# Flamingo gated cross-attention with a mixture of experts: routing of three batches moved into the second layer, expert regions of 2048 rows, the last projection in the last group's gaps, and the first layer's fills dealt anew

## The chip, the cores and the metric

The kernel runs on one core of a Trainium2 chip. The metric is the device time of that core in microseconds (us) for one execution. Lower is better. Everything is in float32.

## What is computed

The stream `x` is 4 batches of 512 tokens of 256 numbers, the context 4 batches of 512 rows of 512 numbers. Each of four parts adds `tanh(gate) * part(layernorm(x))` to the stream. Cut to what matters:

```
x = x + tanh(g_xattn[0]) * _L0_xattn_ref(_layernorm(x), ctx, ...)   # 16 heads of 16, 512 own keys and 512 of the context
x = x + tanh(g_ffn[0])   * _L0_ffn_ref(_layernorm(x), ...)          # 64 units of 16 hidden values, relu
x = x + tanh(g_xattn[1]) * _L1_xattn_ref(_layernorm(x), ctx, ...)   # 16 heads of 64, 512 context keys and a null key; layernorm of the result
x = x + tanh(g_ffn[1])   * _L1_ffn_ref(_layernorm(x), ...)          # 8 experts of width 1024, the best 2 for each token

def _L1_ffn_ref(X, Wg, bg, W1, W2, W3):
    logits = einsum('btd,de->bte', X, Wg) + bg
    topv, topi = top_k(logits, 2);  w = softmax(topv);  xs = X * w        # one scaled row for each choice
    out = X + sum over e of  where(topi == e, (silu(xs @ W1[e]) * (xs @ W3[e])) @ W2[e], 0)
```

## The kernel before, in words

Three functions run one after the other; each is a block in which the five engines have streams of their own that meet at semaphores. PE is the matrix engine, DVE, ACT and POOL the three others, SP issues loads. T is 4, the number of 128-token tiles of a batch.

**`layer0`.** The 16 heads of a batch are worked in quads of 4, 16 quads in all (q = 0 to 15), each in 8 steps (kt) of 2 halves (c). Before a quad's exponentials its row maxima are needed: `max_scores` computes scores into one of two PSUM banks and `take_max` on DVE reads them, 32 times for each quad, so 512 maxima. The first quad's 32 stand ahead of all its scores. In the steps of quad q, PE computes scores (L348), ACT takes exponentials (L474), PE multiplies them with the values (L363), and the maxima of quad q + 1 run between. What else must be done for later quads and for the batch before is a *fill*: projections of queries and keys (`qk`), values (`v`), transposes into the layouts that the scores need (`q`, `k`), transposes of the result (`oT`), the output projection (`out`), the norm's transposes (`xT`, `xT2`), the unit network (`sin`, `ffn`). A table `slots[(q, kt, c)]`, written by rule, says after which half step a fill is issued. A fill's PSUM bank is free when ACT or DVE has read the fill before it. `q = -1`, `-2` and `-3` are the prologue. Norm statistics of batch 1 stand in the prologue, too.

**`layer1`.** 32 groups (i), 8 to a batch, each of two heads, in 4 steps (r). In each step PE issues: scores of the next group, `scores(i + 1, r)`; a fill at `(i, r, 0)`; 8 transposes of this group's probabilities, `transpose_probs(i, r)`; a fill at `(i, r, 1)`; `weigh_values` of the step before. There is one bank for all fills, so each fill waits until ACT (`misc_act`) or DVE (`misc_dve`) has read the one before. The norm of a batch after its attention (`route_tokens`, into `routed_xn`) is spread over later groups for the first three batches. After the last group `project_output` forms the last batch's projection, 8 head pairs and the null key for each of 4 tiles, and DVE does the norm of it (`output_statistics`, `norm_output`), adds it (`add_output`, L1248).

**`experts`.** A first block norms the last batch again (L61 to L87 on `moe_stats`), transposes all 16 tiles (L1515), forms the logits (L1502) and clears `moe_sorted_x`, the DRAM array of rows sorted by expert (23 tiles of 256 rows). A second block ranks the experts for all tiles (L1529 to L1541), counts the rows of each expert with two matmuls and a prefix sum (L1565, L1566), gives each row its slot and adds the residual (L1605), while ACT scales the first choice's rows (L1614). In a third block ACT scales the second choice's rows (L1775), POOL writes 32 blocks of 128 rows to `moe_sorted_x` by indirect DMA (L1856), SP loads weights (L1679, L1681: 3 DMAs to a piece, 8 pieces of slots) and, when the rows are scattered, the first tiles of rows (L1689). Then come 23 tiles of 8 steps; each weight and each row is split in a high and a low part (`hi`, `lo`), and a product is three matmuls (L1726, L1740). Results go to `moe_y` by indirect DMA (L1862), addressed by token and choice. A fourth block loads both results of each token (L1889), adds them to the stream (L1901, L1903) and writes the output (L1913).

## Time and profile before

| | |
|---|---|
| median of the runs | 2056.9 us (3 runs, 2053.74 to 2070.22) |
| the profiled execution | 2059.87 us |
| its span | 2058.2 us, mean granted PE clock 0.938 |
| PE busy | 1794.1 us (87%) |
| DVE, ACT, POOL busy | 1174.3, 1112.4, 435.1 us |
| layer 0 | 0 to about 690 us |
| layer 1 | about 690 to 1523 us |
| routing, scatter, first weights | 1523 to 1616 us |
| expert tiles | 1616 to 2026 us |
| results and output | 2026 to 2058 us |

The profile is of one execution. The span is what the profiler saw, 1.7 us less than the time that the same execution took; other times in the text are positions from the span's start. An engine's busy time counts its compute instructions. Where an engine was idle the profile names what released it.

### The profile page before, as it was taken

What the parts mean: (1) busy time and instruction counts of PE and PEld (TensorE: products, weight loads), DVE (VectorE), ACT (ScalarE), POOL (GpSimd) and SP (SyncE); (2) the same over time, 40 slices, a digit from 0 to 9 for tenths busy, and PEclk for the clock granted to TensorE, in tenths of its full rate; (3) what the DMA queues carried; (4) which work ended last, traced back from release to release, by engine and by line L of the source; (5) the groups of instructions that cost most, each with busy time, mean ns of one, the idle gap of its engine ahead of it and who ended that gap; (6) DMA issues with size and microseconds to landing.
All of it is one profiled execution on the core that took longest, in us unless ns stands there. A gap on an engine that the chain in (4) does not pass through costs nothing. (4 is left out here: it accounts for less than half of the span.)

```text
span 2058.2 us, 27842 instructions
## 1 busy us (share of the span) xinstructions
PE 1794.1 (87%) x9504; PEld 1125.6 (55%) x9504; DVE 1174.3 (57%) x2825; ACT 1112.4 (54%) x2328; POOL 435.1 (21%) x429
## 2 busy tenths in 40 slices
PE   6899998998997599999999999999870699999993
PEld 3455554554543244444444444454360699999993
DVE  4767777776782455545564556445534355555553
ACT  2366665666665255544554455455513477766771
POOL 3010210110101000000000000000013677777761
PEclk8699999999999799999999999999975799999997
DMA  2000000000000400000000000000035566666644
GB/s 92 1 21 1 11 11 1 2 20 1 0 1 1 149 0 1 21 1 0 1 21 1 1 0 21 1 1 1 1 124 176 176 208 213 208 205 208 206 136 136
DMA packets 112109, 122.42 MB, mean 59 GB/s; under 512 B 9249, under 2 KB 105889, under 8 KB 111969
## 3 DMA queue, kind: packets, MB, share of 16 engines
q1 hardware_dynamic: 104944, 107.76, 16.7%
q0 software_dynamic: 3744, 10.49, 1.4%
q10 hardware_dynamic: 3280, 2.40, 0.4%
q8 instruction: 77, 1.26, 0.3%
q14 instruction: 64, 0.52, 0.1%
HBM read 101.63 MB, written 18.99 MB: 59 GB/s over the span
## 5 line engine op out<-in xcount | busy, mean ns | idle before, releaser
L613 DVE TENSOR_REDUCE l_tile_max<-psum 128x1 f32<-128x512 f32 x512 | 343.9, 690 | 114.7 <-PE psum L333 113.3
L474 ACT ACTIVATE l_probs<-psum 128x1024 f32<-128x1024 f32 x256 | 248.2, 1022 | 104.1 <-PE psum L348 99.9
L333 PE MATMUL psum<-l_kT,l_qT 128*128 128x512 f32 x512 | 245.8, 485 | 37.8 <-DVE l_tile_max L613 33.5
L1848 POOL TENSOR_TENSOR moe_w_lo<-moe_w,moe_w_hi 128x512 fp32r<-128x512 f32 x184 | 241.5, 1313 | 116.3 <-ACT moe_w_hi L1766 115.6
L1190 DVE TENSOR_REDUCE l_row_max<-psum 128x2 f32<-128x1024 f32 x128 | 156.5, 1223 | 162.5 <-PE psum L942 162.2
L1102 ACT ACTIVATE l_null_p<-l_s_null,l_neg_max 128x1 f32<-128x1 f32 x256 | 73.8, 288 | 278.9 <-DVE l_neg_max L1192 278.9
L1726 PE MATMUL psum<-moe_xs_hi,moe_w_hi 128*128 128x256 f32 x736 | 210.9, 287 | 1.4 <-DVE moe_xs_lo L1804 1.4
L1726 PE MATMUL psum<-moe_xs_lo,moe_w_hi 128*128 128x256 f32 x736 | 208.9, 284 | 0.0
L1726 PE MATMUL psum<-moe_xs_hi,moe_w_lo 128*128 128x256 f32 x736 | 208.9, 284 | 0.0
L1829 DVE TENSOR_TENSOR psum<-psum,moe_gate 128x256 f32<-128x256 f32 x184 | 79.4, 432 | 165.0 <-ACT moe_gate L1784 165.0
L333 PEld LDWEIGHTS psum<-l_kT,l_qT 128*128 128x128 f32 x512 | 100.9, 197 | 129.7 <-DVE l_tile_max L613 109.6
L1104 ACT ACTIVATE l_probs<-psum,l_neg_max 128x512 f32<-128x512 f32 x256 | 171.7, 671 | 0.0
L348 PE MATMUL psum<-l_qT,l_kT 128*128 128x512 f32 x512 | 162.0, 400 | 1.8 <-ACT l_probs L474 1.7
L1047 PEld LDWEIGHTS psum<-ident,l_probs 128*128 128x128 f32 x1024 | 119.9, 142 | 70.9 <-issue 52.7
L970 PE MATMUL psum<-l_wv,l_ctxT 128*128 128x512 f32 x256 | 129.8, 654 | 20.4 <-ACT l_null_pT L1130 7.3
L942 PE MATMUL psum<-l_k_sb,l_q_sb 64*128 64x512 f32 x512 | 144.7, 642 | 0.0
L1726 PEld LDWEIGHTS psum<-moe_xs_hi,moe_w_hi 128*128 128x128 f32 x736 | 141.9, 193 | 1.8 <-DVE moe_xs_lo L1804 1.8
L1726 PEld LDWEIGHTS psum<-moe_xs_lo,moe_w_hi 128*128 128x128 f32 x736 | 142.0, 193 | 0.0
L1726 PEld LDWEIGHTS psum<-moe_xs_hi,moe_w_lo 128*128 128x128 f32 x736 | 141.8, 193 | 0.0
L1047 PE MATMUL psum<-ident,l_probs 128*128 128x128 f32 x1024 | 134.7, 275 | 7.9 <-DVE l_probs L1204 5.0
L1061 PE MATMUL psum<-l_probsT,l_v_sb 128*64 128x512 f32 x512 | 140.8, 629 | 0.1
L1784 ACT ACTIVATE moe_gate<-psum 128x256 f32<-128x256 f32 x184 | 70.7, 384 | 127.2 <-PE psum L1726 127.2
(245 smaller groups left out, 3234.7 us busy)
## 6 DMA issues: line engine op xcount, KB each, us to landing
moe_w<-in_moe_w SPq DMA_DIRECT2D x276, 256.0 KB, 4.3
moe_sorted_x<-moe_zeros SPq DMA_DIRECT2D x1, 6256.0 KB, 20.5
moe_xs<-moe_sorted_x SPq DMA_DIRECT2D x23, 272.0 KB
l_ctxT<-in_ctxT SPq DMA_DIRECT2D x4, 1024.0 KB, 5.5
x_resid<-in_x SPq DMA_DIRECT2D x4, 512.0 KB, 10.8
l_raw<-in_ctx SPq DMA_DIRECT2D x4, 512.0 KB, 3.6
l_v_raw<-in_ctx SPq DMA_DIRECT2D x4, 512.0 KB, 3.5
l_wk<-in_wkv SPq DMA_DIRECT2D x1, 2048.0 KB, 16.3
```

Of the source, the lines that this page charges most:

```text
L333: nc.tensor.matmul(bank(4 + m % 2), qT[:, q % SLOTS, h, t * P:(t + 1) * P], kT[:, q % SLOTS, h // 2, half * BANK:(half + 1) * BANK], start ...
L348: last = nc.tensor.matmul(bank(2 * (n % 2) + i), kT[:, q % SLOTS, c, kt * P:(kt + 1) * P], qT[:, q % SLOTS, 2 * c + i, :], start=True, sto ...
L474: nc.scalar.activation(probs[:, n % PT_RING], wide(2 * (n % 2)), ACT.Exp, scale=SCALE).then_inc(exp_done, 1)
L613: nc.vector.reduce_max(tile_max[:, q % 2, t, h, half:half + 1], bank(4 + m % 2), AX_X).then_inc(max_read, 1)
L942: last = nc.tensor.matmul(bank(2 * (t % 2) + j), q_sb[head, i % 2, t * P:(t + 1) * P], k_sb[head, i % 2, :], start=True, stop=True)
L970: last = nc.tensor.matmul(bank(MISC), ctxT[:, c, kt * P:(kt + 1) * P], wv[:, c, half * BANK:(half + 1) * BANK], start=(c == 0), stop=(c == ...
L1047: last = nc.tensor.transpose(bank(4 + j)[:, t * P:(t + 1) * P], probs[:, i % 2, t, j, kt * P:(kt + 1) * P], ident[:])
L1061: last = nc.tensor.matmul(bank(O_BANK)[j * DH:(j + 1) * DH, :], v_sb[:, kt, h * DH:(h + 1) * DH], probsT[:, m % 2, j, :], start=(kt == 0), ...
L1104: last = nc.scalar.activation(probs[:, i % 2, t, j, :], bank(2 * (t % 2) + j), ACT.Exp, bias=neg_max[:, t, j:j + 1], scale=SCALE, accum_ou ...
L1190: nc.vector.reduce_max(row_max[:, t, :], wide(2 * (t % 2)).rearrange("p (j m) -> p j m", j=2), AX_X)
L1726: last = nc.tensor.matmul(bank(k % 3)[:, n * ROWS:(n + 1) * ROWS], w, x_part[:, i % 2, c, :], start=(c == 0 and j == 0), stop=(c == s.DC - ...
L1848: nc.gpsimd.tensor_tensor(w13_lo[:, k % SPLITS], w13[:, slot_k, :, cols], w13_hi[:, k % SPLITS].bitcast(F32), ALU.subtract).then_inc(w13_s ...
```

## The change

**Layer 0.** The table is dealt anew: the four `k` fills of a quad move to kt 0, 1, 3, 4, the first `q` fill of quad q + 3 to (q, 7, 0), the `xT`, `qk`, `xT2`, `sin` and the second `out` fill to later half steps; `UNIT_AT` (the unit network on POOL and DVE) starts 2 steps later. The first 32 maxima use six banks in turn, and the prologue's fills two instead of six. The statistics of batch 1 move from the prologue into quad 0. The `v` fills of the prologue come after the first maxima.

**Layer 1.** New fills `rT` (2), `logits` and `prefix` route batches 0, 1 and 2 inside the layer: for batch 0 in groups 15, 16, 17 and 19, for batch 1 in groups 23, 24, 25 and 27, for batch 2 in groups 30 and 31. DVE ranks the experts of one batch at a time, ACT scales its rows, POOL scatters 8 blocks for each batch. Each expert has a region of 2048 rows of `moe_sorted_x`, so a row's slot needs only the running count of its expert (`run`); the array grows from 46 to 130 blocks of 128 rows and is cleared at the start of layer 1. In the last group 7 of 8 head pairs of the projection of tiles 0 to 3 stand between the last steps; the eighth pair and the null key follow after the last `weigh_values`. The last batch's norm, logits and slots follow in the same block, with the output norm in two fused operations for each tile.

**Experts.** The two routing blocks are gone. DVE turns the counts into a list of tiles, each with its expert and its first row (`list_tiles`), before SP may load weights; SP reads a tile's first row from `start_ids`. POOL scatters the last batch's 8 blocks. DVE instead of POOL splits the first five `w13` weights. The loads of the results stand in the same block, behind the wait for the stores of `moe_y` on SP and ACT.

```diff
 # layer0
-    UNIT_AT = ((2, 1), (2, 3), (2, 4), (2, 4), (2, 5), (2, 6), (2, 7), (3, 0))
+    UNIT_AT = ((2, 3), (2, 4), (2, 4), (2, 5), (2, 6), (2, 7), (3, 0), (3, 0))
...
         if 0 <= q + 2 < NQ:
-            slots[q, 0, 0] = ("q", q + 2, 0)
-            for k, at in enumerate(((1, 0), (2, 1), (3, 0), (4, 0))):
-                slots[(q,) + at] = ("k", q + 2, k)
+            slots.update({(q, kt, 0): ("k", q + 2, k) for k, kt in enumerate((0, 1, 3, 4))})
             slots[q, 5, 0] = ("q", q + 2, 1)
...
+        if 0 <= q + 3 < NQ:
+            slots[q, 7, 0] = ("q", q + 3, 0)
...
         if b + 1 < B and r == 0:
-            slots.update({(q, 7, c): ("xT", b + 1, c) for c in range(2)})
+            slots[q, 7 if b == 0 else 2, 1] = ("xT", b + 1, 0)
         if b + 1 < B and r == 1:
-            slots.update({(q, kt, 1): ("qk", b + 1, t) for t, kt in enumerate((0, 3, 4, 5))})
+            slots[q, 0, 1] = ("xT", b + 1, 1)
+            slots.update({(q, 2 + t, 1): ("qk", b + 1, t) for t in range(T)})
         if b + 1 < B and r == 2:
-            slots.update({(q, 3 + h, 1): ("v", b + 1, h) for h in range(2)})
+            slots.update({(q, (5 if b < 0 else 3) + h, 1): ("v", b + 1, h) for h in range(2)})
         if b >= 1 and r == 0:
             slots.update({(q, 3 + c, 1): ("oT", b - 1, c) for c in range(2)})
-            slots.update({(q, 5 + h, 1): ("out", b - 1, h) for h in range(2)})
+            slots.update({(q, 5 + 2 * h, 1): ("out", b - 1, h) for h in range(2)})
         if b >= 1 and r == 1:
-            slots.update({(q, 7, c): ("xT2", b - 1, c) for c in range(2)})
+            slots[q, 7, 1] = ("xT2", b - 1, 0)
         if b >= 1 and r == 2:
-            slots[q, 0, 1] = ("sin", b - 1)
+            slots[q, 0, 1] = ("xT2", b - 1, 1)
+            slots[q, 2, 1] = ("sin", b - 1)
...
-    START_BANKS, TAIL_BANKS = (MISC, O_BANK, 0, 1, 2, 3), (0, 1, 2, 3, 4, 5)
+    START_BANKS, TAIL_BANKS, FIRST_BANKS = (MISC, O_BANK), (0, 1, 2, 3, 4, 5), (4, 5, 0, 1, 2, 3)
...
-                    if r == 3 and b + 2 < B and kt in (1, 3, 4):
+                    if (r == 3 and 0 <= b < B - 2 or q == 0) and kt in (1, 3, 4):
 # layer1
+    for c in range(ROUTED):
+        first = (c + 1) * PAIRS + PAIRS - 1
+        if c + 1 < ROUTED:
+            at = (first, 0, 1), (first + 1, 0, 1), (first + 2, 0, 1), (first + 4, 0, 1)
+        else:
+            at = (first - 1, 1, 0), (first - 1, 1, 1), (first - 1, 2, 0), (first, 1, 0)
+        slots.update(zip(at, (("rT", c, 0), ("rT", c, 1), ("logits", c), ("prefix", c))))
...
+                clear = g["xs_dram"].rearrange("(n p) d -> p n d", p=P)
+                sp.dma_start(clear, zeros[:].unsqueeze(1).to_broadcast([P, clear.shape[1], WIDE])).then_inc(cleared, 16)
...
+                        if i == GROUPS - 1 and r >= 1:
+                            if r == 1:
+                                pe.wait_ge(exp_done, GROUPS * T)
+                                pe.wait_ge(o_read, GROUPS - 1)
+                            project_heads(bank(r - 1)[:, 0:D], s.B - 1, r - 1, range(PAIRS - 1))
                         if i >= 0 and r >= 1:
                             weigh_values(i, r - 1)
...
+                project_heads(bank(T - 1)[:, 0:D], s.B - 1, T - 1, range(PAIRS - 1))
                 weigh_values(GROUPS - 1, KT - 1)
...
                 for t in range(T):
-                    project_output(bank(t)[:, 0:D], s.B - 1, t).then_inc(out_psum, 1)
+                    if t == 0:
+                        pe.wait_ge(o_read, GROUPS)
+                    project_heads(bank(t)[:, 0:D], s.B - 1, t, (PAIRS - 1,))
+                    project_null(bank(t)[:, 0:D], t).then_inc(out_psum, 1)
 # experts
-                    sp.dma_start(xs[:, i % 2], xs_dram[i * ROWS:(i + 1) * ROWS, :].rearrange("(h p) d -> p h d", p=P)
+                    first = sp.value_load(start_ids[0:1, i:i + 1], min_val=0, max_val=E * s.REGION)
+                    sp.dma_start(xs[:, i % 2], xs_dram[bass.ds(first, ROWS), :].rearrange("(h p) d -> p h d", p=P)
...
+                sp.wait_ge(tiles_ready, 1)
                 for m in range(PIECES):
...
+                all_stored(sp)
+                for b in range(NB):
+                    load_results(sp, 0, b)
...
+                list_tiles()
                 for k in range(AHEAD):
                     split_down(k)
+                    slot_k, cols, _ = arrived(k)
+                    dve.wait_ge(w13_rounded, k + 1)
+                    nc.vector.tensor_tensor(w13_lo[:, k % SPLITS], w13[:, slot_k, :, cols],
+                                            w13_hi[:, k % SPLITS].bitcast(F32), ALU.subtract).then_inc(first_split, 1)
```

**How the order moves, at three places.** On PE in the prologue of layer 0, before (L371 are transposes, L414 the values' projection, L333 the scores for the maxima):

```order
3 L371 MATMUL psum<-ident,l_q_stack 128x128 x4
4 L371 MATMUL psum<-ident,l_k_stack 128x128 x12
5 L414 MATMUL psum<-l_w_qkv,l_xT 128x256 x4
6 L371 MATMUL psum<-ident,l_k_stack 128x128 x4
7 L414 MATMUL psum<-l_w_qkv,l_xT 128x256 x4
8 L333 MATMUL psum<-l_kT,l_qT 128x512 x2
9 L371 MATMUL psum<-ident,l_q_stack 128x128 x4
10 L333 MATMUL psum<-l_kT,l_qT 128x512 x12
11 L371 MATMUL psum<-ident,l_q_stack 128x128 x4
12 L333 MATMUL psum<-l_kT,l_qT 128x512 x4
13 L371 MATMUL psum<-ident,l_k_stack 128x128 x4
14 L333 MATMUL psum<-l_kT,l_qT 128x512 x5
```

and in the changed kernel, where the same three are L380, L423 and L345:

```order
3 L380 MATMUL psum<-ident,l_q_stack 128x128 x4
4 L380 MATMUL psum<-ident,l_k_stack 128x128 x16
5 L345 MATMUL psum<-l_kT,l_qT 128x512 x2
6 L380 MATMUL psum<-ident,l_q_stack 128x128 x4
7 L345 MATMUL psum<-l_kT,l_qT 128x512
8 L423 MATMUL psum<-l_w_qkv,l_xT 128x256 x4
9 L345 MATMUL psum<-l_kT,l_qT 128x512 x4
10 L423 MATMUL psum<-l_w_qkv,l_xT 128x256 x4
11 L345 MATMUL psum<-l_kT,l_qT 128x512 x3
12 L380 MATMUL psum<-ident,l_q_stack 128x128 x4
13 L345 MATMUL psum<-l_kT,l_qT 128x512 x4
14 L380 MATMUL psum<-ident,l_k_stack 128x128 x4
```

Both projections of values now stand behind the first maxima.

On PE in layer 1, group 15, the first of the new fills; before, where L942 are scores, L951 a `q` fill, L1047 the transposes of probabilities and L1061 the weighing:

```order
1276 L1061 MATMUL psum<-l_probsT,l_v_sb 64x512 x2
1277 L942 MATMUL psum<-l_k_sb,l_q_sb 128x512 x2
1278 L951 MATMUL psum<-l_xT,l_wq 128x512 x2
1279 L1047 MATMUL psum<-ident,l_probs 128x128 x8
1280 L1061 MATMUL psum<-l_probsT,l_v_sb 64x512 x2
1281 L942 MATMUL psum<-l_k_sb,l_q_sb 128x512 x2
```

and in the changed kernel, where these are L1000, L1009, L1139 and L1153:

```order
1285 L1153 MATMUL psum<-l_probsT,l_v_sb 64x512 x2
1286 L1000 MATMUL psum<-l_k_sb,l_q_sb 128x512 x2
1287 L1009 MATMUL psum<-l_xT,l_wq 128x512 x2
1288 L1139 MATMUL psum<-ident,l_probs 128x128 x8
1289 L1075 MATMUL psum<-ident,routed_rows 128x128 x4
1290 L1153 MATMUL psum<-l_probsT,l_v_sb 64x512 x2
```

The four transposes of `routed_rows` (L1075) follow the `q` fill with only the 8 transposes between; both use the one bank for fills.

On PE in the last group and behind it, before, from the last group's second transposes (L1006 and L1007 are the projection's head pairs and null key, 8 and 1 to a tile):

```order
1552 L1047 MATMUL psum<-ident,l_probs 128x128 x8
1553 L1061 MATMUL psum<-l_probsT,l_v_sb 64x512 x2
1554 L1047 MATMUL psum<-ident,l_probs 128x128 x8
1555 L1061 MATMUL psum<-l_probsT,l_v_sb 64x512 x2
1556 L1001 MATMUL psum<-ident,l_null_cols 128x128 x4
1557 L1047 MATMUL psum<-ident,l_probs 128x128 x8
1558 L1061 MATMUL psum<-l_probsT,l_v_sb 64x512 x4
1559 L1006 MATMUL psum<-l_wo,l_oT 128x256 x8
1560 L1007 MATMUL psum<-l_w_null_v,l_null_pT 128x256
1561 L1006 MATMUL psum<-l_wo,l_oT 128x256 x8
1562 L1007 MATMUL psum<-l_w_null_v,l_null_pT 128x256
1563 L1006 MATMUL psum<-l_wo,l_oT 128x256 x8
```

and in the changed kernel (L1064 and L1067 are the projection; the routing of the last batch follows it in the same block):

```order
1579 L1139 MATMUL psum<-ident,l_probs 128x128 x8
1580 L1064 MATMUL psum<-l_wo,l_oT 128x256 x7
1581 L1153 MATMUL psum<-l_probsT,l_v_sb 64x512 x2
1582 L1059 MATMUL psum<-ident,l_null_cols 128x128 x4
1583 L1139 MATMUL psum<-ident,l_probs 128x128 x8
1584 L1064 MATMUL psum<-l_wo,l_oT 128x256 x7
1585 L1153 MATMUL psum<-l_probsT,l_v_sb 64x512 x2
1586 L1064 MATMUL psum<-l_wo,l_oT 128x256 x7
1587 L1153 MATMUL psum<-l_probsT,l_v_sb 64x512 x2
1588 L1064 MATMUL psum<-l_wo,l_oT 128x256
1589 L1067 MATMUL psum<-l_w_null_v,l_null_pT 128x256
1590 L1064 MATMUL psum<-l_wo,l_oT 128x256
```

28 of the 32 head-pair matmuls (7 to a tile) now stand between the last group's transposes and weighings, and one pair to a tile behind.

## Rows read from the trace of the kernel before

**Rows 1.** Busy time by window; DMA share and GB/s last.

```profile
core 0: us, PE busy (x) PEld busy (x) DVE busy (x) ACT busy (x) POOL busy (x), PEclk, DMA share, GB/s
38.30:86.00 47.70, 37.40 (x95) 21.77 (x94) 38.09 (x77) 11.10 (x18) 7.65 (x11) 0.57 0.00 0
1140.00:1330.00 190.00, 184.07 (x739) 86.92 (x738) 100.71 (x270) 96.63 (x239) 5.99 (x8) 0.99 0.02 6
1576.00:1584.00 8.00, 0.00 (x0) 0.00 (x0) 1.38 (x4) 2.86 (x7) 6.04 (x7) 0.50 1.08 384
```

**Rows 2.** Waits of PE over the span: us in total, times, longest.

```profile
PE psum L1712 <- DMA moe_xs<-moe_sorted_x: 60.5, 1, 60.5
PE psum L371 <- DVE l_o_tok L658: 9.6, 14, 1.1
PE psum L427 <- DVE l_qT L627: 3.9, 3, 1.3
```

**Rows 3.** Timeline of PE, layer 0: start us, us, instruction, idle before.

```profile
33.38 3.12 PE L414 MATMUL psum<-l_w_qkv,l_xT 128*128 128x256 f32 x8
...
38.32 0.82 PE L333 MATMUL psum<-l_kT,l_qT 128*128 128x512 f32 x2
...
81.23 1.06 PE L348 MATMUL psum<-l_qT,l_kT 128*128 128x512 f32 x2
```

**Rows 4.** The page, costliest groups: busy, mean ns, idle before.

```profile
L613 DVE TENSOR_REDUCE l_tile_max<-psum 128x1 f32<-128x512 f32 x512 | 343.9, 690 | 114.7 <-PE psum L333 113.3
```

**Rows 5.** Timeline of PE in layer 1, groups 14 to 24.

```profile
1059.08 0.66 PE L978 MATMUL psum<-ident,l_rows 128*128 128x128 f32 x4
...
1063.44 1.11 PE L978 MATMUL psum<-ident,l_rows 128*128 128x128 f32 x4 [2.84 <-ACT l_xT L1126]
...
1082.14 1.96 PE L986 MATMUL psum<-l_w_null,l_xT 128*128 128x16 f32 x16
```

**Rows 6.** Timeline around 1450: transposes on PE, the fill read by ACT.

```profile
1448.86 1.04 PE L1047 MATMUL psum<-ident,l_probs 128*128 128x128 f32 x8
...
1450.37 0.59 ACT L1119 ACTIVATE l_q_sb<-psum 128x512 f32<-128x512 f32 x1
```

**Rows 7.** Timeline of DVE in group 30: maxima of consecutive steps.

```profile
1466.74 1.22 DVE L1190 TENSOR_REDUCE l_row_max<-psum 128x2 f32<-128x1024 f32 x1
...
1476.31 1.22 DVE L1190 TENSOR_REDUCE l_row_max<-psum 128x2 f32<-128x1024 f32 x1
```

**Rows 8.** Timeline of PE and DVE behind the last group.

```profile
1497.98 3.69 PE L1006 MATMUL psum<-l_wo,l_oT 128*128 128x256 f32 x16 [0.74 <-issue]
...
1513.86 1.43 DVE L61 BATCH_NORM_STATS2 l_out_stats<-psum 128x6 f32<-128x256 f32 x4 [27.94 <-PE psum L1007]
...
1544.10 0.29 DVE L1485 TENSOR_TENSOR moe_logits<-psum,moe_b_router 128x128 f32<-128x128 f32 x1 [3.73 <-PE psum L1502]
```

**Rows 9.** Groups of DVE, 1498 to 1568: busy us, mean ns, idle before.

```profile
L1536 DVE TENSOR_TENSOR moe_cmp<-moe_cmp,moe_tie 128x1024 f32<-128x1024 f32 x1 | 1.2, 1226 | 0.1
```

**Rows 10.** Timeline at the start of the experts: SP, POOL, PE.

```profile
1568.39 0.91 SPq L1679 DMA_DIRECT2D moe_w<-in_moe_w  x2
...
1608.20 0.96 POOL L1856 DMA_INDIRECT moe_sorted_x<-routed_xn,moe_slot_ids  x1 [0.30 <-issue]
...
1610.65 0.88 SPq L1689 DMA_DIRECT2D moe_xs<-moe_sorted_x  x2
...
1616.01 0.58 PE L1726 MATMUL psum<-moe_xs_hi,moe_w_hi 128*128 128x256 f32 x1 [1.41 <-DVE moe_xs_lo L1804]
```

**Rows 11.** Timeline at the end: the last store and results loads.

```profile
2028.09 0.96 POOL L1862 DMA_INDIRECT moe_y<-moe_y_sb,moe_places  x1 [0.31 <-issue]
...
2037.36 2.83 SPq L1889 DMA_DIRECT2D moe_first_rows<-moe_y  x4
```

**Rows 12.** DMA issues: count, KB each, median us to landing.

```profile
moe_sorted_x<-moe_zeros SPq DMA_DIRECT2D x1, 6256.0 KB, 20.5
...
moe_y<-moe_y_sb,moe_places POOLq DMA_INDIRECT x46, 2.5
```

More of the change, by code:

```diff
@@ L820, in layer1 @@
         slots.update({(i, 3, y): fill for y, fill in late.items()})
+    for c in range(ROUTED):
[5 more added lines that the diff above has]
+        slots.update(zip(at, (("rT", c, 0), ("rT", c, 1), ("logits", c), ("prefix", c))))
     def read_by_dve(fill):
-        return fill[0] in ("k", "null") or fill[0] == "xT" and fill[2] == 1
+        return fill[0] in ("k", "null", "logits", "prefix") or fill[0] == "xT" and fill[2] == 1
     fills = [slots[at] for at in sorted(slots)]
@@ L1159, in _ @@
                             keep_result(i - 1)
+                        route(i, r)
                 keep_result(GROUPS - 1)
+                act.wait_ge(last_psum, 1)
+                nc.scalar.activation(rT[:, 0, :], bank(4), ACT.Copy).then_inc(last_act, 1)
+                weigh_second(s.B - 1)
+                for k in range(TOP):
+                    scale_rows(s.B - 1, k, range(T))
             @block.gpsimd
@@ new lines, in choose_slots, with add_residual @@
+                def choose_slots(c):
+                    dve.wait_ge(scattered, 16 * TOP * T * c)
+                    dve.drain()
+                    for k in range(TOP):
+                        nc.vector.tensor_tensor(chosen[:, k], chosen[:, k], work8[:], ALU.mult)
+                    dve.drain()
+                    nc.vector.reduce_sum(slot[:], chosen[:], AX_X)
+                    dve.drain()
+                    nc.vector.tensor_copy(slot_ids[:], slot[:]).then_inc(slots_ready, 1)
+                def add_residual(c, some):
+                    for t in some:
+                        x_t = tokens(c)[:, t, :]
+                        last = nc.vector.scalar_tensor_tensor(out=x_t, in0=routed[:, t, :], scalar=gates[:, 3:4], in1=x_t,
+                                                              op0=ALU.mult, op1=ALU.add)
+                    if some[-1] == T - 1:
+                        last.then_inc(residual_added, 1)
@@ L1219, in read_fill @@
                         last = nc.vector.tensor_copy(xT[:, rest[1], :], bank(MISC))
+                    elif kind == "logits":
+                        last = add_router_bias(bank(MISC))
+                    elif kind == "prefix":
+                        last = add_counts(rest[0], bank(MISC))
                     else:
@@ L1408, in experts @@
-        row_places = sb("row_places", [P, TILES, HALVES])
+        start_ids = sb("start_ids", [P, TILES], U32)
         places = sb("places", [P, 3, HALVES], U32)
-        rows = (first_rows, xn)
+        results = [sb(f"results_{k}", [P, T, D]) for k in range(TOP)]
         w13 = sb("w13", [P, W_SLOTS, 2 * s.DC, PIECE * P])
         w2 = sb("w2", [P, W_SLOTS, PIECE, D])
-        stats = sb("stats", [P, TB, 6])
-        mv = sb("mv", [P, TB, 2])
-        work = sb("work", [P, 4, TB])
-        norm = Norm(nc, TB, stats, mv, work)
@@ L1771, in round_rows @@
                                          ACT.Copy).then_inc(xs_rounded, 1)
-                for t in range(T):
-                    nc.scalar.activation(xn[:, t, 0:D], xn[:, t, 0:D], ACT.Copy,
-                                         scale=weight[:, 1, t:t + 1]).then_inc(second_scaled, 1)
                 for k in range(AHEAD):
@@ L1791, in _ @@
                         round_rows(i + 1)
+                all_stored(act)
+                for b in range(NB):
+                    load_results(act, 1, b)
             @block.vector
@@ L1840, in _ @@
                 evacuate_y(TILES - 1)
+                for b in range(NB):
+                    dve.wait_ge(results_loaded[b], 16 * TOP)
+                    nc.vector.tensor_tensor(block_rows(results[0], b), block_rows(results[0], b), block_rows(results[1], b),
+                                            ALU.add)
+                    dve.drain()
+                    nc.vector.scalar_tensor_tensor(out=block_rows(g["x"], b), in0=block_rows(results[0], b),
+                                                   scalar=g["gates"][:, 3:4], in1=block_rows(g["x"], b), op0=ALU.mult,
+                                                   op1=ALU.add).then_inc(fin, 1)
             @block.gpsimd
@@ L1935, in flamingo @@
         layer0(nc, s, g, bank, wide, dram)
-        g["routed"] = sb("routed_xn", [P, s.T, s.D + ROW_PAD])
+        g["rows"] = [sb(f"routed_rows_{k}", [P, s.TT, s.D + ROW_PAD]) for k in range(TOP)]
+        g["slot_ids"] = sb("slot_ids", [P, TOP, s.TT], U32)
+        g["run"] = sb("run", [P, s.T + 1, s.E])
+        g["first_slot"] = sb("first_slot", [P, s.E])
+        g["tile_no"] = sb("tile_no", [P, s.TILES])
+        g["steps"] = sb("steps", [P, s.MOST])
+        g["row_places"] = sb("row_places", [P, s.TILES, ROWS // P])
+        g["scattered"] = ctx.enter_context(nc.semaphore("rows_scattered"))
+        xs_dram = nc.dram_tensor("moe_sorted_x", [s.E * s.REGION + ROWS, s.D + ROW_PAD], F32).ap()
+        g["xs_dram"] = xs_dram
         layer1(nc, s, g, bank, wide, dram)
```

625 lines of the change are left out of this document (345 added, 280 removed).

## The prediction

> **What bounds the kernel now.** I read the table of windows first, then PE's waits, then the timeline at each place that the diff touches. PE is busy 87% of the span, so the question is where it is not. Three stretches are PE-bound: layer 0 from 86 us on, layer 1, and the expert tiles. In layer 1 PE is busy 184.07 of 190 us at a granted clock of 0.99 [rows 1]: there an added PE instruction costs its full length, a removed wait gives its full length. Three stretches are not. At the start of layer 0, between the first maxima and the first scores, PE runs at a clock of 0.57 and DVE is busy 38.09 of 47.7 us [rows 1]; both are near their limit. Between the last group and the first expert tile PE works little, and one wait for the first sorted rows is 60.5 us [rows 2]: this is the largest thing in the profile. At the end PE is done by 2026 us and the span goes on to 2058 us.
>
> **The change part by part.** Sums are against the profiled execution, 2059.87 us, which is 3.0 above the median of 2056.9; I come back to that.
>
> *1. Start of layer 0.* Before, 8 of the values' matmuls stood ahead of the first maxima in two runs; the first was 3.12 us beside 4 transposes [rows 3]. They now follow the first three maxima, where PE is filled up to DVE's pace anyway, so the first maximum comes about 3 us sooner. From 38.32 to the first scores at 81.23 [rows 3] were 42.9 us, in which DVE takes 42 maxima at 0.69 us [rows 4] = 29, casts keys and queries (about 4), and computes statistics for batch 1, some 5 us of small instructions. The statistics leave, so DVE needs about 33, and with 6 banks instead of 2 in the ring the two engines hardly wait for each other. PE at its low clock needs about as much. I take 34: 8.9 off, and 3 from the earlier start, less 2.4 given back in quad 0, where the statistics now stand beside maxima at full pace: **−9.5**. Bounds: −14 with nothing given back, −4 if the cold PE sets the pace as before.
>
> *2. Layer 0 in steady state.* PE waits 14 times for DVE's normalised result (L658), 9.6 us in total, since a `tok` fill's reading stands ahead of the next fill; 3 times 1.3 us for `l_qT` before an `out` fill [rows 2]; and about ten times half a microsecond for ACT's copy of a `q` fill before a `qk` or `sin` fill. The new table moves a `k` or a `q` fill away from behind each: I count 7 × 0.65 us, 7 × 0.5, and 3 × 0.8. Against them, the `q` fill that moves to (q, 7, 0) meets DVE's cast and a copy: +2. Sum **−8.4**, bounds −12 and 0 (all waits return elsewhere, since the work of a fill is unchanged and only its neighbours differ).
>
> *3. Fills of batches 0 and 1 in layer 1.* Added to a PE-bound stretch. Work: four transposes took 0.49 us (1059.08 to the next instruction) and sixteen small matmuls 1.81 [rows 5], so a batch costs 2 × 0.49 for `rT`, 1.81 for `logits` and 0.45 for `prefix`: 3.24 us. Waits: each new fill stands at (i, 0, 1) behind a `q` fill with one set of transposes between. PE ended such a set at 1449.9, while ACT read the `q` fill only from 1450.37 for 0.59 us [rows 6], so the new fill could begin only some 1.3 to 1.5 us later. I take 1.4 for all four. Two batches: 2 × (3.24 + 4 × 1.4) = **+17.7**. Bounds: +6.5 without waits; +30 if each wait is like the 2.84 us between two adjacent `xT` fills, after which the next four transposes took 1.11 us instead of 0.66 [rows 5]. I stay nearer the low one because transposes stand between. DVE, ACT and POOL get about 12, 5 and 12 us for each batch, spread over five groups in which they are half idle [rows 1]; free, as long as a probability's chain is not late.
>
> *4. Groups 30 and 31.* Here the last maxima come 4.79 us apart [rows 7], set by the chain maxima, exponentials, normalisation and the small norm steps on DVE, and not by PE; batch 2's fills lie in PE's idle time, but ranking and slots on DVE do not: **+2.6**. In the last group PE is already nearly full. Each tile's 8 pairs took 3.62 to 3.69 us [rows 8], so 7/8 of four tiles = 12.7 us move in front of the last weighing and only 2 to 3 us of idle time is there to be filled, minus slower issue: **−0.8**. This part does hardly anything.
>
> *5. From the projection's end to the first weight load.* Before: 1513.86 [rows 8] to 1568.39 [rows 10], 54.5 us. First the norms, transposes and logits, 30.2 us to 1544.10 [rows 8]. Now: output statistics 4.9, two fused operations for each tile 3.6 (before 4.5), statistics 4.9 with no block's end and no copy before them (some 6 us saved), norm 1.4, no wait for the logits of the other 12 tiles (2.3 saved), transposes, copies and logits 7.0: 21.8, so −8.4. Then 24.2 us of ranks, sums, slots and residual for 16 tiles. The long ranking operations took 1.23 us for 1024 elements [rows 9] and are five; for 256 elements I take 0.5 with the drain: 2.6. Compare 0.9, running counts 1.25, slots 0.95, weights 0.75, residual 1.6, ACT's second scaling behind it 1.6, block's end 0.4, tile list 4.0 and SP's read of it 0.9: 15.0 to 15.6, −8.9. Together **−17.3** (bounds −13, −20).
>
> *6. First weight load to first expert product.* Before: 1568.39 to 1616.01, 47.6 us, set by 32 scatters on POOL, the last at 1608.20; the rows' load at 1610.65 follows and takes 5.4 us to the first product [rows 10]. Now 8 scatters take 10 us and the path is SP's: rows are loaded behind 24 weight loads of 256 KB on the same queue. 6.3 MB and 1.1 MB of scatters at the 384 GB/s of the busiest window [rows 1] are 19.3 us, plus about 4 of ramp, plus 2 for the rows and 2.5 for transposes and split: 27.8. **−19.8**. Bounds: −29 if rows needn't wait for the weights (10.1 + 2.5 + 5.4), −13 if the queue is slower. The new loads from a register's address have no row; weight loads are addressed so already, I add nothing.
>
> *7. Expert tiles.* The same 184 steps of 2.16 us: 0. Splits moved from POOL to DVE are done before the rows arrive.
>
> *8. End.* The last store is issued at 2028.09; a store lands 2.5 us after its issue [rows 12], the loads of the results are issued at 2037.36 [rows 11], after POOL's wait and a block's end. Now SP and ACT wait for the stores themselves: loads at 2030.6, **−6.7** (bounds −1, −7).
>
> *9. The clear of `moe_sorted_x`* grows from 6256 KB, which took 20.5 us [rows 12], to 17,680 KB: 58 us at that pace, but at the start of layer 1, where the DMA engines are all but idle once its weights are in; the next user is batch 1's context. 0, if it doesn't delay `wk`, ahead of it in the queue.
>
> Sum: −9.5 − 8.4 + 17.7 + 2.6 − 0.8 − 17.3 − 19.8 − 6.7 = −42.2, so 2017.7 for the profiled execution, 2014.7 from the median. Forecast **2016**.
>
> **The rivals.**
>
> *A. PE's clock falls in layer 1.* The eight new waits may each be followed by slow instructions, as the 2.84 us wait was (1.11 for 0.66 us [rows 5]). At 1.3 us each: +10, so 2026. Against it: waits of 1.47 us and less were not followed by slow rows in layer 0. The Trainium skill says in "TensorE: Matmul & The Clock Gate", section "A second HAM failure mode: psum-queue depth-cycling", that frequent short idles between matmul groups can make the clock swing; the trace agrees only for waits of over 1.6 us. Chance 0.2.
>
> *B. Start and steady state of layer 0 give nothing*, because cold PE sets the start and waits move to other fills. For it: clock 0.57 [rows 1]. Against: DVE busy 38.09 of 47.7. +14, so 2030. Chance 0.12.
>
> *C. The start of the experts is held by the queue.* Rows behind 24 weight loads and a read of the expert list for each piece; half of term 6 is lost: 2026. The Trainium skill ("DMA: Bandwidth & Descriptors", "Queues, rings and completion order") says that an engine takes turns among queue rows by packets, so scatters and weights share and neither stands still; by it POOL's 8 scatters would not be the delay, while rows on SP's own row still queue. No row here separates the two. Chance 0.1.
>
> *D. Slower than before.* Layer 1's step is PE-bound, so if each new wait left PE at half clock for about half a group (a group is 19.4 us) it would cost 5 us more. It decides from 42/8 = 5.3 us for each of the eight: +48, 2064. Against it: after the 2.84 us wait only the next row or two were slow. Chance 0.03.
>
> *E. The change doesn't do what it says:* the last group has no gaps worth the name (term 4), already in the sum.
>
> **How the numbers follow.** The forecast's own case has 0.55, its bounds put it at 2003 to 2028; A, B and C lie at 2026 to 2030. Cases together (A with B) reach 2036. The range of 8 in 10 is 2001 to 2034. Here 1% (20.6 us) is about what a measurement can tell from no change: faster by more, below 2036, has 0.91; within 1% 0.06; slower 0.03.
>
> **What would show it.** Right: the stretch between the last weighing and the first expert product falls from 119 to about 70 us; PE's wait for the first sorted rows is about 40 us; first scores near 70 us; eight waits of 1.3 to 1.5 us in groups 15 to 27, and a layer 1 that is 15 to 20 us longer up to group 30; results loads about 2 us after the last store. Wrong: a granted clock in layer 1 below 0.95; waits for `l_tile_max` in layer 0 that grow by what the others lost; exponentials late behind the ranking in groups 18 and 26; more than 35 us from the first weight load to the first product.

## The result, and the profile after

The changed kernel takes 2037.9 us (median of 4, 2030.95 to 2043.6), the kernel before 2055.6 (4, 2053.74 to 2070.22): ratio 0.9903, interval 0.988 to 0.9926. So it is 1% faster, 18 to 20 us, where 41 were forecast; the time lies above the range's end of 2034. The profiled execution took 2036.1, its span is 2034.4: 23.8 less than the profiled one of before. 6 us of that difference are the two executions' own: the one of before was 4.3 above its median, this one is 1.8 below.

The table of windows of the changed kernel, beside [rows 1]:

```profile
core 0: us, PE busy (x) PEld busy (x) DVE busy (x) ACT busy (x) POOL busy (x), PEclk, DMA share, GB/s
38.00:86.00 48.00, 37.31 (x163) 23.26 (x161) 41.90 (x78) 19.69 (x27) 7.57 (x11) 0.89 0.00 1
1140.00:1330.00 190.00, 181.00 (x720) 86.47 (x719) 102.46 (x287) 94.30 (x233) 14.40 (x18) 0.96 0.04 12
1580.00:1588.00 8.00, 0.00 (x0) 0.00 (x0) 3.78 (x8) 2.69 (x6) 0.00 (x0) 0.50 1.09 365
```

In the start of layer 0 PE's granted clock is 0.89 and no longer 0.57 (in other executions it is lower, as the experiments show). In layer 1's window PE is busy 181.00 of 190 us instead of 184.07. The weights still load at 365 GB/s. PE's waits, beside [rows 2]:

```profile
PE psum L345 <- DVE l_tile_max L622: 37.6, 37, 2.6
PE psum L1832 <- DMA moe_xs<-moe_sorted_x: 35.6, 1, 35.6
PE psum L1075 <- DVE routed_rows L93: 14.8, 1, 14.8
PE psum L380 <- POOL l_k_stack L600: 5.3, 7, 2.4
PE psum L1075 <- ACT l_q_sb L1227: 4.4, 4, 1.1
PE psum L1075 <- ACT l_rT L1240: 3.1, 1, 3.1
PE psum L380 <- DVE l_o_tok L667: 2.3, 3, 1.0
```

The wait for the first sorted rows fell from 60.5 to 35.6 us, that for `l_o_tok` from 9.6 to 2.3 (another 3.8 us now stand at two other lines). New are the waits of the routing fills (L1075) for `l_q_sb` and for `l_rT`; the one of 14.8 us is the last batch's, whose first transposes now stand in this block behind its norm. The wait for `l_tile_max`, which was 33.5, is 37.6.

Layer 0's start, beside [rows 3]: first maxima at 33.65 instead of 38.32, first scores at 67.43 instead of 81.23.

```profile
33.65 0.73 PE L345 MATMUL psum<-l_kT,l_qT 128*128 128x512 f32 x2 [0.69 <-ACT l_kT L501]
...
67.43 1.00 PE L357 MATMUL psum<-l_qT,l_kT 128*128 128x512 f32 x2
```

Batch 2's second transposes in group 30, and the first transposes of group 31:

```profile
1490.58 0.90 PE L1075 MATMUL psum<-ident,routed_rows 128*128 128x128 f32 x4 [3.09 <-ACT l_rT L1240]
...
1505.37 1.97 PE L1139 MATMUL psum<-ident,l_probs 128*128 128x128 f32 x8 [3.57 <-DVE l_probs L1394]
```

Then the places of [rows 8, 10, 11]: the output statistics, the first weight load, the rows' load and the first expert product, the last store and the loads of the results.

```profile
1535.12 1.42 DVE L67 BATCH_NORM_STATS2 l_out_stats<-psum 128x6 f32<-128x256 f32 x4 [20.72 <-PE psum L1067]
...
1571.69 0.91 SPq L1790 DMA_DIRECT2D moe_w<-in_moe_w  x2
...
1589.32 1.51 SPq L1801 DMA_DIRECT2D moe_xs<-moe_sorted_x  x2
...
1598.26 0.58 PE L1846 MATMUL psum<-moe_xs_hi,moe_w_hi 128*128 128x256 f32 x1 [1.41 <-DVE moe_xs_lo L1923]
...
2011.09 0.96 POOL L2025 DMA_INDIRECT moe_y<-moe_y_sb,moe_places  x1 [0.30 <-issue]
...
2013.50 1.48 SPq L1760 DMA_DIRECT2D moe_results<-moe_y  x3
```

Laid side by side, the positions (us from the span's start) give where the 23.8 us came from. A quad's or a group's "scores" are its first ones, and a quad's last step is the first scores of its kt 7:

| stretch | before | changed | difference | forecast |
|---|---|---|---|---|
| start to scores of quad 1 | 111.5 | 101.2 | −10.2 | −9.5 |
| to quad 15's last step | 529.8 | 529.1 | −0.7 | −8.4 |
| to layer 1's first scores | 68.9 | 74.2 | +5.3 | 0 |
| to the scores of group 31 | 753.5 | 775.0 | +21.5 | +17.7 |
| to the output statistics | 50.2 | 55.7 | +5.5 | +1.8 |
| to the first weight load | 54.5 | 36.5 | −18.0 | −17.3 |
| to the first expert product | 47.7 | 26.6 | −21.1 | −19.8 |
| to the end | 442.1 | 436.1 | −6.0 | −6.7 |

Below the fifth row everything is as forecast. The miss is in layers 0 and 1: +21.4 against +1.6 forecast. How much of it is the change and how much one execution was the question for the experiments.

### The profile page after: what moved, and what is told of

It is laid out like the page before. It is cut to its first block and busy times, and to the rows that moved or that the text cites. A ratio compares the mean times of both kernels' runs of the same rounds, so it can differ in the third digit from the quotient of the medians.

```text
span 2034.4 us, 28113 instructions
## 1 busy us (share of the span) xinstructions
PE 1792.8 (88%) x9516; PEld 1121.3 (55%) x9516; DVE 1181.5 (58%) x2893; ACT 1116.2 (55%) x2334; POOL 423.8 (21%) x430
## 5 line engine op out<-in xcount | busy, mean ns | idle before, releaser
L345 PE MATMUL psum<-l_kT,l_qT 128*128 128x512 f32 x512 | 236.2, 469 | 40.9 <-DVE l_tile_max L622 37.6
L2013 POOL TENSOR_TENSOR moe_w_lo<-moe_w,moe_w_hi 128x512 fp32r<-128x512 f32 x179 | 233.2, 1303 | 139.6 <-ACT moe_w_hi L1886 138.9
L345 PEld LDWEIGHTS psum<-l_kT,l_qT 128*128 128x128 f32 x512 | 98.1, 192 | 131.4 <-DVE l_tile_max L622 110.3
L1139 PEld LDWEIGHTS psum<-ident,l_probs 128*128 128x128 f32 x1024 | 120.4, 142 | 65.5 <-issue 53.6
L1000 PE MATMUL psum<-l_k_sb,l_q_sb 64*128 64x512 f32 x512 | 147.0, 651 | 0.0
L1153 PE MATMUL psum<-l_probsT,l_v_sb 128*64 128x512 f32 x512 | 141.7, 632 | 0.0
L1139 PE MATMUL psum<-ident,l_probs 128*128 128x128 f32 x1024 | 134.8, 275 | 5.7 <-DVE l_probs L1394 5.3
## 6 DMA issues: line engine op xcount, KB each, us to landing
moe_sorted_x<-l_zeros SPq DMA_DIRECT2D x1, 17680.0 KB, 57.1
```

The costliest lines, as they stand in the source:

```text
L345: nc.tensor.matmul(bank(max_bank(m)), qT[:, q % SLOTS, h, t * P:(t + 1) * P], kT[:, q % SLOTS, h // 2, half * BANK:(half + 1) * BANK], sta ...
L1000: last = nc.tensor.matmul(bank(2 * (t % 2) + j), q_sb[head, i % 2, t * P:(t + 1) * P], k_sb[head, i % 2, :], start=True, stop=True)
L1139: last = nc.tensor.transpose(bank(4 + j)[:, t * P:(t + 1) * P], probs[:, i % 2, t, j, kt * P:(kt + 1) * P], ident[:])
L1153: last = nc.tensor.matmul(bank(O_BANK)[j * DH:(j + 1) * DH, :], v_sb[:, kt, h * DH:(h + 1) * DH], probsT[:, m % 2, j, :], start=(kt == 0), ...
L2013: nc.gpsimd.tensor_tensor(w13_lo[:, k % SPLITS], w13[:, slot_k, :, cols], w13_hi[:, k % SPLITS].bitcast(F32), ALU.subtract).then_inc(w13_s ...
```

## The experiments

All times are medians; "the changed kernel" is 2037.9. The kernels of one group ran on one chip beside the kernel before (2055.2, 2058.1 and 2058.4 there; 2060.9, once, beside the changed kernel taken again), so medians of different groups compare to within some 3 us only.

**Layer 0 as before.** The function `layer0` of the kernel before in the changed kernel.

```diff
-def layer0(...):   # the changed one
+def layer0(...):   # the one of before, word for word
```

> The changed kernel with layer 0 as in the kernel before, all else as changed. Theory 1 (all of layer 0's gain is its start: first scores 13.8 us earlier in the trace, 10.2 us of it left at quad 1, and the dealing anew of the later fills is worth 0 to 1 us): the layer reaches the scores of quad 1 at 111 us and of quad 15 at about 615, as before, and the kernel takes 10 to 11 us more than the changed one, about 2048. Rival (the later fills are worth the 8 us that I forecast, and the clock in the tail hid it): 18 us more, about 2056.

2036.1 (2033.76 to 2042.06, ratio 0.9926, 0.9897 to 0.9955, where the changed kernel has 0.9903): not slower by anything that the scatter lets one see. Scores of quad 1 came at 107.9, of quad 15 at 617.2, and layer 1's first scores at 704.1, against 101.2, 611.1 and 704.5. Neither theory had this: in these two traces, the 6.6 us that the new layer 0 has at quad 1 are gone when layer 1 begins.

**The new start, with the later fills as before.**

```diff
-    for q in range(-QUADS, NQ):      # the new table
+    for q in range(-QUADS, 0):       # the new table, q + 3 only for quads 0 and 1
...
+    for q in range(0, NQ):           # the table of before, UNIT_AT and the places in `piece` too
```

> The changed kernel with the new prologue of layer 0, but the fills of quads 0 to 15, the unit network's steps and the places of the output projection's reading dealt as in the kernel before. Theory 1: same as the changed kernel within 2 us, the distance from quad 1 to quad 15 within 1 us of it. Rival: 8 us more, all of it between quad 1 and quad 15.

2039.9 (2033.85 to 2044.68), the same within 2 us. From quad 1 to quad 15's last step 528.9 us with the old table, 529.1 in the changed kernel. That pair hides a little: six of the eight traces of the new layer 0 have 526.3 to 526.5 there, and the one above and the kernel with layer 0 as before, in its two variants, 528.9, 527.8 and 527.9. So the later fills are worth 1.3 to 2.6 us, not 8. The waits say why. Of the kernel with layer 0 as before, in 110 to 630 us:

```profile
PE psum L339 <- DVE l_tile_max L619: 24.7, 25, 2.3
PE psum L377 <- DVE l_o_tok L664: 8.4, 13, 0.7
PE psum L433 <- DVE l_qT L633: 3.9, 3, 1.3
```

and of the changed kernel:

```profile
PE psum L345 <- DVE l_tile_max L622: 28.7, 28, 2.3
PE psum L418 <- DVE l_o_tok L667: 1.9, 3, 0.7
PE psum L444 <- DVE l_o_tok L667: 1.9, 3, 0.7
PE psum L380 <- DVE l_o_tok L667: 1.3, 2, 0.7
```

The waits for DVE's result and for DVE's `l_qT` went from 12.3 to 5.1 us, and the wait for `l_tile_max` rose from 24.7 to 28.7: PE gets sooner to maxima whose bank DVE has not read yet. DVE does the same maxima in the same order, so more than half of what the fills don't wait the maxima do.

**The old start, with the new later fills,** the complement.

```diff
+    for q in range(-QUADS, 0):       # the table of before
...
+    slots[-1, 7, 0] = ("q", 2, 0)    # joins the old table for q < 0 to the new one from q = 0
...
-    START_BANKS, ..., FIRST_BANKS = (MISC, O_BANK), ..., (4, 5, 0, 1, 2, 3)
+    START_BANKS, ... = (MISC, O_BANK, 0, 1, 2, 3), ...   # and batch 1's statistics in the prologue
```

> The changed kernel with the start of layer 0 as before (fills of the prologue, six fill banks, two banks for the maxima, batch 1's statistics in the prologue) and the new dealing from quad 0 on: the complement of the run with the old later fills. Three runs with the new dealing took 74 to 75 us from quad 15's last step to layer 1's first scores, three with the old one 68 to 69, with the same PE instructions in between. Theory 4 (the dealing of the later fills decides when the clock falls in the tail): 74 to 75 us again, and the kernel is about 6 us slower than the changed one with layer 0 of before, 2042. Rival (it is where the tail falls in time, which the start sets): 68 to 69 us and the distance from quad 1 to quad 15's last step at 525 to 529, 2035.

2043.6 (2040.2 to 2048.22): 73.1 us in the tail and 2042 forecast by theory 4, so it looked right. Two kernels of the same group took that back, the one with the head pairs behind the last group and the one with two banks: both have the new dealing, and the tail took 68.9 and 68.6 us. Why this kernel reaches layer 1's first scores at 713.3, the latest of all traces, stays open.

**Two banks for the first maxima.**

```diff
-    ..., FIRST_BANKS = ..., (4, 5, 0, 1, 2, 3)
+    ..., FIRST_BANKS = ..., (4, 5)
```

> The changed kernel with two banks instead of six for the first 32 maxima. Theory 7 (the start was gained by the values' fills and the statistics leaving, and DVE sets the pace): from the first maximum to the first scores 33.8 to 35 us as in the changed kernel. Rival (the hand-over between PE and DVE on two banks was the cost): 37 to 40 us, 3 to 6 more.

From the first maximum to the first scores 41.6 us, in the changed kernel 33.8: 7.8 more, above the rival's 3 to 6 as well. With the old layer 0 it is 40.4 to 42.9. DVE is busy 29.8 us of the 41.6, in the changed kernel 28.8 of the 33.8, so DVE's busy time doesn't set the length. That the hand-over does is not shown, because the granted clock differs too: 0.64 in this start, 0.90 in the changed kernel's. PE is busy 33.5 us instead of 23.7 with the same instructions, while its waits for maxima are 6.1 us instead of 5.3. The changed kernel's two other executions, below, lie between: 37.3 and 37.0 us at 0.73 and 0.78. Whether two banks bring the clock down, or this execution drew a low one, one trace can't tell. The kernel takes 2035.6, no more than the changed one: what the start loses is made up before layer 1, as in the first experiment.

**The changed kernel again, twice.**

> The changed kernel once more, for its trace. Theory 10 (the same instructions meet the clock at another point each time): scores of quad 0, of quad 1 and the tail from quad 15's last step to layer 1's first scores differ between executions of one kernel, as they did between kernels with the same layer 0 (67.4 to 72.1, 101.2 to 107.1 and 68.6 to 75.4 us), and the tail is either near 69 or near 74. Rival (the kernel's own): 67.4, 101.2 and 74.2 within 0.5 us each time.

> The changed kernel a third time, for its trace: as the one before.

2039.9 and 2038.6. First scores at 72.6 and 72.0, scores of quad 1 at 107.6 and 107.1, the tail 68.8 and 68.6 us, where the first execution had 67.4, 101.2 and 74.2. All three numbers differ between executions of one kernel. All traces, in us:

| | first scores | quad 1 | tail | layer 1's first scores |
|---|---|---|---|---|
| old layer 0: before | 81.2 | 111.5 | 68.9 | 710.1 |
| layer 0 as before | 76.9 | 107.9 | 68.4 | 704.1 |
| all three edits, layer 0 as before | 77.5 | 107.9 | 68.7 | 704.5 |
| new layer 0: changed, three times | 67.4, 72.6, 72.0 | 101.2, 107.6, 107.1 | 74.2, 68.8, 68.6 | 704.5, 702.8, 702.0 |
| late fills; rows early | 68.1, 68.1 | 103.0, 103.1 | 75.2, 75.4 | 704.5, 704.8 |
| batch 2 later; heads behind | 67.4, 72.1 | 101.3, 107.1 | 74.1, 68.9 | 704.6, 702.6 |
| all three edits | 70.7 | 105.8 | 68.8 | 700.9 |
| new start, later fills as before | 70.6 | 106.4 | 68.8 | 704.1 |
| old start, new later fills | 80.6 | 112.3 | 73.1 | 713.3 |
| two banks | 75.0 | 110.1 | 68.6 | 705.0 |

Eight traces of the new layer 0 (the last three rows are mixtures) reach layer 1's first scores at 703.3 in the mean, three of the old at 706.2. So the new dealing is worth about 3 us, of 17.9 forecast, and perhaps less: without the trace of the kernel before, at 710.1, the old ones have 704.3. The tail has two lengths, 68 to 69 and 73 to 75. The four traces whose first scores came by 68.1 all have the long one, the five others with the new start and the new later fills (the one with two banks among them) the short one, so what an execution gains early it has lost again by layer 1. In both PE runs the same instructions, at another granted clock (windows of the tail of the changed kernel, the first execution and the second):

```profile
630.00:704.00 74.00, 40.39 (x116) 21.50 (x112) 28.28 (x80) 13.69 (x19) 8.28 (x23) 0.63 0.42 143
```

```profile
634.00:703.00 69.00, 35.31 (x118) 18.55 (x116) 28.34 (x80) 13.52 (x20) 8.31 (x23) 0.73 0.42 144
```

```profile
638.50 6.57 PE L436 MATMUL psum<-l_w_proj,l_oT 128*128 128x256 f32 x16 [0.80 <-ACT l_oT L527]
```

```profile
642.23 3.69 PE L436 MATMUL psum<-l_w_proj,l_oT 128*128 128x256 f32 x16 [0.83 <-ACT l_oT L527]
```

The same output projection takes 6.57 us in the one and 3.69 in the other.

**The routing fills 1 us later.**

```diff
-                        fill((i, r, 1))
+                        routing = slots.get((i, r, 1), ("",))[0] in ("rT", "logits", "prefix") and r == 0
+                        if not routing:
+                            fill((i, r, 1))
...
                         elif i >= 1:
                             weigh_values(i - 1, KT - 1)
+                        if routing:
+                            fill((i, r, 1))
```

> The changed kernel with the eight routing fills at (i, 0, 1) of batches 0 and 1 issued behind weigh_values of the same step instead of ahead of it, 1 us later. Theory 2 (each fill costs a wait of 1.1 to 1.4 us for the read of the q fill, beside 0.5 to 1.8 us of work): the waits shrink to 0.1 to 0.4 us each, layer 1 is 8 to 9 us shorter up to group 30, 2029. Rival (the read of the new fill is then late for the k fill that follows, or the cost is the slower clock): 0 to 2 us less.

2030.2 (2027.31 to 2032.74), 7.7 less, where theory 2 had 8 to 9. In the changed kernel the steps with a new fill are longer than the same steps before by 1.8, 1.8, 3.1 and 1.7 us, for batch 0 as for batch 1: 16.7 together. Here they are longer by 0.8, 0.7, 2.0 and 0.7, 8.6 together, and the step behind `prefix` is longer by 0.5 to 0.9 us. In both kernels the step behind `logits` is longer too, by 1.2 to 1.7 us: in 17 of 20 cases in the ten traces with the fills where the change has them, in 6 of 6 with the late ones. The changed kernel, then this one, at batch 0's `logits` (L1081) and the scores of the next step:

```profile
1146.74 1.95 PE L1081 MATMUL psum<-l_w_router,l_rT 128*128 128x8 f32 x16 [1.10 <-ACT l_q_sb L1227]
...
1149.68 2.08 PE L1000 MATMUL psum<-l_k_sb,l_q_sb 64*128 64x512 f32 x4
```

```profile
1148.84 1.95 PE L1081 MATMUL psum<-l_w_router,l_rT 128*128 128x8 f32 x16
...
1150.72 1.74 PE L1000 MATMUL psum<-l_k_sb,l_q_sb 64*128 64x512 f32 x4
```

Here `logits` waits for nothing, and the four scores behind it take 1.74 us instead of 1.13, in the changed kernel 2.08. So that step is slow behind 16 matmuls of 8 columns each, wait or no wait. It is the clock: with the late fills the step takes 6.50 to 6.55 us at a mean granted clock of 0.74, all six times, and before it took 4.86 and 4.85 at 1.00. Why it falls there stays open. Adding this step, the eight fills cost 18.3 us in three traces of ten and 19.8 to 19.9 in seven, and 13.3 when they are late. That is 5 to 6.6 us less; the rest of the 7.7 is scatter.

**Batch 2's routing one step later.**

```diff
-            at = (first - 1, 1, 0), (first - 1, 1, 1), (first - 1, 2, 0), (first, 1, 0)
+            at = (first - 1, 1, 0), (first - 1, 2, 0), (first - 1, 3, 0), (first, 2, 0)
...
-                        if at == (6, 3):
+                        if at == (7, 0):
                             rank_experts()     # compare_tops, weigh_tops, choose_slots a step later too
```

> The changed kernel with the second transpose, the logits and the prefix of batch 2 one step later (30,2,0), (30,3,0), (31,2,0), and ranking, comparing, weighing and slots one step later too. Theory 5 (groups 30 and 31 grew because the second transpose waits 3.1 us for ACT's copy and the ranking delays the probabilities of group 31): from the scores of group 31 to the first output statistics 2 to 3 us less than 55.7. Rival (DVE's chain is what it is, wherever the ranking stands): within 1 us.

2026.8 (2019.87 to 2029.36). From group 31's scores to the output statistics 48.6 us, 7.1 less than the changed kernel and 1.7 less than before; the median is 11 less, more than this stretch explains. The two waits, of 3.09 and 3.57 us above, shrink to 1.03 and 0.41, and PE is slow behind neither for as long:

```profile
1490.63 0.66 PE L1075 MATMUL psum<-ident,routed_rows 128*128 128x128 f32 x4 [1.03 <-ACT l_rT L1240]
...
1500.75 1.24 PE L1139 MATMUL psum<-ident,l_probs 128*128 128x128 f32 x8 [0.41 <-DVE l_probs L1394]
```

**The head pairs behind the last group.**

```diff
-                            project_heads(bank(r - 1)[:, 0:D], s.B - 1, r - 1, range(PAIRS - 1))
...
-                    project_heads(bank(t)[:, 0:D], s.B - 1, t, (PAIRS - 1,))
+                    project_heads(bank(t)[:, 0:D], s.B - 1, t, range(PAIRS))
```

> The changed kernel with all 8 head pairs of the last batch's projection behind the last weighing, as before. Theory 6 (the last group has no gap to speak of, term 4 of the prediction): the stretch from group 31's scores to the output statistics within 1 us of the changed kernel's 55.7, the kernel the same. Rival (the pairs fill waits of the last group): 3 to 6 us longer.

60.3 us from group 31's scores to the output statistics, in one trace; nine traces with the changed kernel's code there have 54.4 to 57.7, 56.1 in the mean. So the pairs are worth 3 to 6 us: the rival is right. The time (2037.4) doesn't show it. Part of the gain is not a filled gap: behind a wait of 1.08 us the first tile's 16 records take 5.38 us here, the next ones 3.62.

```profile
1519.94 5.38 PE L1064 MATMUL psum<-l_wo,l_oT 128*128 128x256 f32 x16 [1.08 <-ACT l_oT L1256]
...
1525.59 3.62 PE L1064 MATMUL psum<-l_wo,l_oT 128*128 128x256 f32 x16
```

**The first rows after four weight pieces.**

```diff
-                    if m == W_SLOTS:
+                    if m == W_SLOTS // 2:
                         sp.wait_ge(scattered, 16 * TOP * T)
                         load_rows(0)
+                    if m == W_SLOTS:
                         load_rows(1)
```

> The changed kernel with the first tile's rows loaded after 4 weight pieces of 3 DMAs instead of after 8. Theory 3 (rows wait behind weights on SP's queue, scatters are done by 1579): first expert product 6 to 8 us earlier after the first weight load (26.6 us in the changed kernel), then 19 to 20; 2031. Rival (the DMA engines' total rate sets the arrival of the weights that the first steps need, or the rows land no sooner): 0 to 2 us less.

2024.6 (2022.21 to 2028.83), 13 less. From the first weight load to the first product 17.8 us instead of 26.6: 8.8 less, a little more than theory 3 has. The ratio, 0.986 against 0.9903, makes it 8.8 as well; its other stretches are the changed kernel's, so the rest of the 13 is taken for scatter. SP now waits for the scatters, not the rows for the weights:

```profile
1578.80 0.38 SPq L1792 DMA_DIRECT2D moe_w<-in_moe_w  x1
...
1582.74 0.38 SPq L1801 DMA_DIRECT2D moe_xs<-moe_sorted_x  x1
```

**All three edits together, with the new and with the old layer 0.**

> The changed kernel with three edits that each gained by itself: the routing fills of batches 0 and 1 behind weigh_values, batch 2's routing a step later, the first rows loaded after 4 weight pieces. Theory 8 (they are at three different places and add up): 7 + 7 + 8.8 = 23 us less than the changed kernel, 2013 to 2018. Rival (the time gained in layer 1 is partly given back by the clock elsewhere): 2020 to 2026.

> The same three edits with layer 0 as in the kernel before. Theory 9 (in the end layer 0's new dealing is worth nothing that can be measured: 6 us gained by quad 1, given back up to layer 1's first scores): the same as its neighbour within 4 us. Rival (it is worth most of what the first traces showed at quad 1, 6 to 10 us, and one unlucky tail hid it): 7 to 10 us slower than its neighbour.

2011.0 (2002.91 to 2018.38, ratio 0.9769, 0.9739 to 0.9799) and 2013.2 (2011.97 to 2018.23, 0.978, 0.9758 to 0.9802). They add up: the first is 27 us under the changed kernel, where 23 were expected. With layer 0 as before it is 2.2 us more, within the scatter: theory 9. The first of the two is the fastest kernel of this study, 2.3% under the kernel before.

## Why the prediction was wrong

The direction was right, the size was not: 18 to 20 us came of 41. By its own terms:

- **Terms 1 and 2, layer 0, −17.9.** This is the step that failed: both gains were sized too large and let stand to the end. What the runs showed in their place is about −3, in the means of eight traces of the new layer 0 and three of the old. *Term 1, −9.5:* the first scores came at 69.8 instead of 78.5, −8.7, but quad 0 gave back 4 us and not 2.4, so −4.5 is left at quad 1. I also took DVE's busy sum for what sets the start, with PE at its low clock only as long. The run with two banks has the new kernel's DVE work and the old start's length, so it is not that; hand-over or PE's clock stays open. *Term 2, −8.4:* −1.4 from quad 1 to quad 15's last step. I added up the waits that the new table takes away without asking what is late next. DVE's reading of the maxima is: of the 7.2 us gone at the fills 4.0 came back at L345 [rows 4], and PE waits for the POOL's `k_stack` too. The bound that I gave, 0 ("all waits return elsewhere"), was nearer than the value.
- **The tail of layer 0, 0.** I gave it no term. It was +5.3 in the profiled execution and +3.1 in the mean, since four of the eight traces with the new layer 0 have 5 to 7 us more and four none. These three make up the −3.
- **Term 3, +17.7.** The size and its parts were about right: 16.7, with waits of 1.1 us and not 1.4. What I left out is the slow step behind `logits`, +1.6 in the profiled execution and +3.1 in most others. The rest of the trace's +21.5 is mostly slow steps behind waits that both kernels have (the `xT` fills, [rows 5]); from layer 1's first scores on it is −2.1 to +5.0 us from trace to trace.
- **Term 4, +1.8.** +5.5 (+4.2 to +7.5 in the nine traces with this code), of two errors with opposite signs. The pairs in the last group are worth 3 to 6 us and not 0.8. Batch 2's routing costs about 10 (60.3 − 50.2, without the pairs, one trace each) and not 2.6: I priced the ranking on DVE and not the 3.09 us that the second transpose waits until ACT has read the first out of the one bank for fills, nor the slow PE instructions that can follow.
- **Terms 5, 6 and 8.** −18.0, −21.1 and −6.0 to −7, forecast −17.3, −19.8 and −6.7. The gap of 60.5 us was read rightly, down to what bounds it next: the rows behind the weights on SP's queue, which the early rows confirm.
- **Terms 7 and 9.** 409.5 us of expert tiles before, 410.2 after (first product to the start of the last). The clear of 17,680 KB took 57.1 us; from layer 1's first scores to group 15 were 356.2 and 356.1 us. In the other traces, all with the larger clear, it is 353.3 to 360.1, so a cost of 2 or 3 us would not show; neither has one that does.
- **The rivals.** B (layer 0 gives nothing), at 2030 with 0.12, was nearly the case: with term 4's miss of 3.7 added it is 2034, with the slow step behind `logits` 2037. A is there at `logits` alone, 3 us and not 10, and not behind the waits that it was to come from. C was counted in term 6 already and gave no more. D and E did not happen.

The range's upper end should have held B and term 4's miss together; it held each alone.

## What to carry to other kernels

A table of waits is no table of gains: before a wait is counted as gained, name what holds the same engine next, and if another wait on the same partner stands a few instructions on, count little (here 1.4 us of 8.4). A stretch with one long wait and idle engines can be summed from durations to within 2 us, and that is where the gain was. Where a single trace shows a few microseconds won or lost at an engine's start-up, take the trace of the same kernel again before explaining it.

## What the runs showed of the hardware

- One kernel's clock is granted differently from execution to execution over the same instructions: the tail of layer 0 took 69 us at a mean of 0.73 or 74 us at 0.63, and the stretch from the first maximum to the first scores 33.8 us at 0.90, 37.0 at 0.78 or 37.3 at 0.73. What decides it stays open. The dealing of the fills alone does not, since the changed kernel itself shows both lengths; whether it makes the long one likelier (5 of 10 traces with the new later fills, 0 of 4 with the old) the runs are too few to say.
- The step behind the `logits` fill (16 matmuls of 8 columns) ran at a mean granted clock of 0.74 though nothing waited, 6 times of 6, and took 6.5 us instead of 4.9. The four transposes behind a wait of 1.1 us ran at full pace (0.66 us). Behind waits of 2.9 us they did so in some traces and not in others.
- Eight indirect writes beside the weight loads, in the kernel with the early rows: the last was issued at 1575.8, and SP, which waited for them, went on at 1582.7; the stores at the end landed 2.5 us after their issue [rows 12].
